# Position scores written to the shift buffer in two halves per unit, and output stores issued by GpSimd

## The reference

```python
xn  = layernorm(x)
out = x + attention(xn) + mlp(xn)

# attention: 16 heads of width 8, with its own layer norm (ln_g, ln_b)
content = einsum('bihd,bjhd->bhij', q + u_bias, k)
pos     = relative_shift(einsum('bihd,jhd->bhij', q + v_bias, p))   # p = sinusoidal_pe(512) @ Wp
attn    = softmax((content + pos) * 8 ** -0.5)
head    = einsum('bhij,bjhd->bihd', attn, v); return head @ Wo + bo

# relative_shift: pad a zero column in front, read the rows of S+1 numbers as one stream, skip the first S of it
padded = concatenate([zeros(B, H, S, 1), pos_score], -1).reshape(B, H, S + 1, S)
return padded[:, :, 1:].reshape(B, H, S, S)

# mlp: three products with weights +1 or -1 (from booleans), relu between, scales s0, s1, s2
h = relu(s0 * [x, -x] @ K0) * 2; h = relu(s1 * h @ K1) * 2; return s2 * h @ K2
```

## Time and profile before

| what | value |
|---|---|
| median of 3 runs | 1502.39 us (1499.39 to 1502.62) |
| profiled execution's own time | 1495.67 us |
| its span, first to last instruction | 1493.8 us |
| mean granted TensorE clock | 0.969 |
| busy: PE, DVE, ACT, POOL | 93%, 86%, 78%, 46% of the span |
| moved by DMA | 575.12 MB, 98,719 packets, mean 385 GB/s |

### The profile page before, as it was taken

How to read it: one execution, slowest core, us unless ns; L and a number is a source line. 1 busy time by engine, 2 the same in 40 slices (tenths; PEclk the granted TensorE clock), 3 DMA queues, 4 the chain that set the end, 5 groups by cost and what they waited for, 6 DMA issues and landing times.

```text
span 1493.8 us, 40812 instructions
## 1 busy us (share of the span) xinstructions
PE 1384.0 (93%) x15848; PEld 940.0 (63%) x15848; DVE 1289.7 (86%) x3479; ACT 1169.9 (78%) x1272; POOL 683.3 (46%) x919
## 2 busy tenths in 40 slices
PE   4898999989899898989999899998989999898997
PEld 2466666666566666656666666666667666666664
DVE  4698898989799898989989899898989989888885
ACT  3687888878688887878878787887878878787863
POOL 5563544535454463544635453463544535443300
PEclk8699999999999999999999999999999999999999
DMA  3999999999999999999999999999999999999991
GB/s 116 363 420 413 384 410 402 406 408 394 378 394 411 399 408 388 410 409 384 409 392 416 396 401 408 385 406 389 409 408 395 415 400 412 382 406 410 389 414 58
DMA packets 98719, 575.12 MB, mean 385 GB/s; under 512 B 15456, under 2 KB 16224, under 8 KB 32992
## 3 DMA queue, kind: packets, MB, share of 16 engines
q1 hardware_dynamic: 42800, 277.83, 47.4%
q10 hardware_dynamic: 37296, 269.51, 44.5%
q0 software_dynamic: 18432, 25.19, 5.7%
HBM read 274.14 MB, written 273.15 MB: 366 GB/s over the span
## 4 chain that ended last, share of the span: by engine, by line
PE 65%; DMA 22%; ACT 6%; issue 2%; DVE 2%; ACTq 1%; POOL 1%; POOLq 0%
PE ps_pt L701 26%; DMA shift<-pos_sb 21%; PE ps_av L715 12%; PE ps_job L646 11%; PE ps_pos L682 10%; ACT pt_sb L456 4%; ACT pos_sb L446 2%; PE ps_job L625 1%; PE ps_job L616 1%; PE ps_job L611 1%; ACTq L433 1%; PE ps_job L621 1%; PE ps_job L607 1%; DMA sc_sb<-shift 1%; DVE sc_sb L581 1%
## 5 line engine op out<-in xcount | busy, mean ns | idle before, releaser
L581 DVE CUSTOM_DVE_ANT_0 sc_sb<-ps_con,sc_sb 128x512 f32<-128x512 f32 x1024 | 664.8, 684 | 135.0 <-PE ps_con L692 124.6
L446 ACT COPY pos_sb<-ps_pos 128x1024 f32<-128x1024 f32 x510 | 519.0, 1018 | 241.8 <-PE ps_pos L682 155.2
L701 PE MATMUL ps_pt<-c_sb,sc_sb 128*128 128x128 f32 x4096 | 566.6, 282 | 31.6 <-ACT pt_sb L456 18.2
L456 ACT ACTIVATE pt_sb<-ps_pt 128x1024 f32<-128x1024 f32 x512 | 526.1, 1028 | 45.5 <-PE ps_pt L701 45.1
L589 DVE TENSOR_SCALAR sc_sb<-sc_sb,nmax 128x512 f32<-128x512 f32 x1024 | 555.8, 575 | 0.1
L701 PEld LDWEIGHTS ps_pt<-c_sb,sc_sb 128*128 128x128 f32 x4096 | 446.3, 142 | 165.8 <-issue 88.1
L341 POOL CAST h<-act_sb 128x512 fp32r<-128x512 f32 x128 | 78.5, 613 | 541.2 <-ACT act_sb L422 541.0
L715 PE MATMUL ps_av<-pt_sb,v_sb 128*9 128x128 f32 x8192 | 321.9, 275 | 0.6 <-ACT pt_sb L456 0.6
L682 PE MATMUL ps_pos<-p_stack,q_stack 32*128 32x512 f32 x1024 | 263.6, 505 | 58.1 <-ACT pos_sb L446 51.5
L715 PEld LDWEIGHTS ps_av<-pt_sb,v_sb 128*9 128x9 f32 x8192 | 173.3, 90 | 157.8 <-issue 147.7
L692 PE MATMUL ps_con<-k_stack,q_stack 32*128 32x512 f32 x1024 | 262.6, 501 | 0.0
(11 more groups left out here) (85 smaller groups left out, 702.1 us busy)
## 6 DMA issues: line engine op xcount, KB each, us to landing
shift<-pos_sb SPq DMA_DIRECT2D x256, 1026.0 KB, 11.0
sc_sb<-shift ACTq DMA_DIRECT2D x256, 1024.0 KB, 11.0
q_stack<-q_hl POOLq DMA_DIRECT2D x192, 64.0 KB, 7.5
k_stack<-k_hl POOLq DMA_DIRECT2D x192, 64.0 KB, 7.6
x_sb<-in_x SPq DMA_DIRECT2D x16, 256.0 KB, 14.8
out<-x_sb SPq DMA_DIRECT2D x16, 256.0 KB, 13.8
c_sb<-in_consts ACTq DMA_DIRECT2D x1, 517.0 KB, 4.5
sc_sb<-in_wp ACTq DMA_DIRECT2D x1, 256.0 KB, 5.1
```

Of the source, the lines that this page charges most:

```text
L446: act.copy(to, ps_pos[:, :, :]).then_inc(s_pe, 1)
L456: act.activation(pt_sb[:, 2 * i:2 * i + 2, :], ps_pt[:, :, :], ACT.Exp, scale=-1.0) \
L581: dve.tensor_tensor_reduce(sc_sb[:, m % N_SC, t, :], ps_con[:, k, :], sc_sb[:, m % N_SC, t, :], -SCALE, 3.4e38, ALU.add, ALU.min, nmax[:, ...
L701: last = pe.transpose(ps_pt[:, j % 2, t * P:(t + 1) * P], sc_sb[:, u % N_SC, t, j * P:(j + 1) * P], id_sb)
```

## The change

SP writes each unit in two transfers of two places each: the first (places 0 and 1) as soon as half step 2n+1 is copied, the second (places 2 and 3) one step later, at the time at which the whole unit was written before. In a step the second half of unit n-1 is issued ahead of the first half of unit n. There are two semaphores for each room of `pos_sb`, one for each half; ACT waits for both before it reads a unit back, and for one of them before it fills place 0 or place 2 again. The stores of the output go from SP to GpSimd's program (`store`), at half step 2 of the batch after next, ahead of the spread of k, and the last one at the end. `load_x` stays on SP, with its wait for the store.

```diff
--- before.py
+++ after.py
@@ -145,7 +145,7 @@
         s_ps = sem("s_ps")
         s_pos, s_con = sem("s_pos"), sem("s_con")
         s_pe = sem("s_pe")
-        s_out_w = [sem(f"s_pout{i}") for i in range(N_POS)]
+        s_out_w = [[sem(f"s_pout{i}_{k}") for k in range(2)] for i in range(N_POS)]
         s_in = [sem(f"s_in{i}") for i in range(N_SC)]
         s_ttr = sem("s_ttr")
         s_sub = sem("s_sub")
@@ -262,6 +262,18 @@
                 sp.dma_start(x_sb[:, b % N_X].rearrange("p t d -> p (t d)"), chunks(x[b].rearrange("s d -> (s d)"))) \
                   .then_inc(s_x[b % N_X], 16)
 
+            def write(u, k):
+
+                if not 0 <= u < UNITS:
+                    return
+                if u >= N_SHIFT:
+                    v = u - N_SHIFT
+                    sp.wait_ge(s_in[v % N_SC], 16 * (v // N_SC + 1))
+                part = slice(2 * k * PITCH, 2 * (k + 1) * PITCH)
+                sp.dma_start(chunks(shift[u % N_SHIFT])[:, :, part],
+                             pos_sb[:, u % N_POS, 2 * k:2 * k + 2].rearrange("p t c -> p (t c)")) \
+                  .then_inc(s_out_w[u % N_POS][k], 16)
+
             load_x(0)
             for dst, src in ((k0_u8, k0), (k1_u8, k1), (k2_u8, k2)):
                 sp.dma_start(dst, src.rearrange("(a p) n -> p a n", p=P)).then_inc(s_wb, 16)
@@ -269,24 +281,12 @@
 
             for n in STEPS:
                 it, slot = n // 16, n % 16
-                if it >= 2 and slot == 1:
-                    sp.wait_ge(s_jev, job("TY", it - 2))
-                    sp.dma_start(chunks(out[it - 2].rearrange("s d -> (s d)")),
-                                 x_sb[:, (it - 2) % N_X].rearrange("p t d -> p (t d)")).then_inc(s_out, 16)
                 if 0 <= it and it + 2 < B and slot == 4:
                     load_x(it + 2)
-                u = unit(n, 1)
-                if u is not None:
-                    sp.wait_ge(s_pe, score_halves(2 * u + 3))
-                    if u >= N_SHIFT:
-                        v = u - N_SHIFT
-                        sp.wait_ge(s_in[v % N_SC], 16 * (v // N_SC + 1))
-                    sp.dma_start(chunks(shift[u % N_SHIFT]),
-                                 pos_sb[:, u % N_POS].rearrange("p t c -> p (t c)")) \
-                      .then_inc(s_out_w[u % N_POS], 16)
-            sp.wait_ge(s_jev, job("TY", B - 1))
-            sp.dma_start(chunks(out[B - 1].rearrange("s d -> (s d)")),
-                         x_sb[:, (B - 1) % N_X].rearrange("p t d -> p (t d)")).then_inc(s_out, 16)
+                if 0 <= n <= UNITS:
+                    sp.wait_ge(s_pe, score_halves(2 * n + 1))
+                    write(n - 1, 1)
+                    write(n, 0)
             sp.wait_ge(s_out, 16 * B)
 
         @block.gpsimd
@@ -353,6 +353,11 @@
                 for third, part in enumerate(thirds):
                     pool.dma_start(stack[third:P:4, g, :], hl[32 * g:32 * g + 32, part, :]).then_inc(landed[g], 16)
 
+            def store(b):
+                pool.wait_ge(s_jev, job("TY", b))
+                pool.dma_start(chunks(out[b].rearrange("s d -> (s d)")),
+                               x_sb[:, b % N_X].rearrange("p t d -> p (t d)")).then_inc(s_out, 16)
+
             scales(0)
             pool.wait_ge(s_c, 16)
             for h in HALVES:
@@ -363,6 +368,8 @@
                     if h == -8:
                         pool.wait_ge(s_fill, 2)
                     spread(h // 8 + 1, QS, q_hl, (0, 0, 1), s_qh, s_q)
+                if h % 32 == 2 and 2 <= h // 32 <= B:
+                    store(h // 32 - 2)
                 if h % 8 == 2:
                     spread(h // 8, KS, k_hl, (0, 1, 0), s_kh, s_k)
                 if h == 5:
@@ -374,6 +381,7 @@
                 b = batch_at(h, NORM_Z)
                 if b is not None:
                     norm(b, 1)
+            store(B - 1)
 
         @block.scalar
         def _(act):
@@ -428,7 +436,8 @@
             for h in HALVES:
                 u, i = half_of(h, SHIFT_H)
                 if i == 0:
-                    act.wait_ge(s_out_w[u % N_POS], 16 * (u // N_POS + 1))
+                    act.wait_ge(s_out_w[u % N_POS][0], 16 * (u // N_POS + 1))
+                    act.wait_ge(s_out_w[u % N_POS][1], 16 * (u // N_POS + 1))
                     wait(act, s_pt, 2 * (u - N_SC + 1))
                     act.dma_start(sc_sb[:, u % N_SC].rearrange("p t c -> p (t c)"),
                                   chunks(shift[u % N_SHIFT, S:S + S * S])) \
@@ -437,8 +446,8 @@
                 if todo:
                     act.wait_ge(s_pos, score_halves(h))
                     for u, t in todo:
-                        if t == 0 and u >= N_POS:
-                            act.wait_ge(s_out_w[u % N_POS], 16 * (u // N_POS))
+                        if t % 2 == 0 and u >= N_POS:
+                            act.wait_ge(s_out_w[u % N_POS][t // 2], 16 * (u // N_POS))
                     to = [pos_sb[:, u % N_POS, t, 1:PITCH] for u, t in todo]
                     if len(to) == 2:
                         to = bass.AP(tensor=to[0].tensor, offset=to[0].offset,
```

## The result

The changed kernel takes 1720.58 us (median of 4 runs, 1718.87 to 1725.99) against 1501.72 us for the kernel before beside it (median of 4). The ratio of all runs is 1.1466, 95% interval 1.1437 to 1.1495. That is 219 us slower; forecast were 23.

A forecast was written before the change was run, and what follows sets the result against it. The prediction took the DMA engines' time as the bound. Its terms, 25 - 3 + 1 = +23 us on the profiled 1495.67, gave 1518.7, about 1525 us as a median of runs; range 1488 to 1558 us.

The forecast's parts named there:

- Packets: the term that decides: Halved writes on SP's queue add 36,864 packets at 11 ns each over 16 engines: +25 us, bounds 0 and 46.
- Packets cost more: Rival: packets cost 20 to 27 ns, as writes from and to odd addresses; +46 to +62, 1546 to 1562 us, chance 0.14.
- the bound: DMA engines' time is the kernel's length from about 45 to about 1460 us; more DMA time lengthens it one for one.
- for a DMA share of 1 nothing more can be moved: In the steady stretches, share 1.02 or 1.03 at 394 to 404 GB/s, the engines were taken to be at their limit.
- a shorter wait at full engines gives nothing: ACT's wait for a unit's write may shorten, but at constant DMA time that does not shorten the kernel.
- the prediction's estimate with it: Per-packet overhead plus extra access for starts off 256 B: 3.5 to 13 ns a packet, a sum of 8 to 30 us.
- the rival with a transfer's fixed part: Rival: each write's fixed 2.1 us shows, 256 x 2.1 = 538 us if nothing hid it; 2040 us, chance 0.01.
- its 512 issues: SP's 256 more issues of 0.518 us, 133 us, fit beside 1262 us of waiting: cost 0 while the backlog covers it.
- a store held it: Each of 16 stores holds GpSimd some 0.5 to 2.1 us, covered by its waits: cost 0, plus 1 us at the end.
- The ends: At start and end of the kernel, half writes going sooner save time: -3 us, bounds 0 to -5.
- its named wait: ACT's waits for the write of `shift` from `pos_sb` were to go up by some 20 us.
- It becomes faster: Rival: at ACT's stall before the copy, long writes stand in the way; halving them gives 1472 us, chance 0.15.

The follow-up runs named there:

- aligned halves: Kernel before with each unit's write cut into two transfers at the old time, pieces of 4,096 B at multiples of 4,096 B: 1531.74 us against 1526.62.
- pieces of 4,112 B: Kernel before with two transfers of two places at the old time, row pitch 514 numbers, gapless, starts at multiples of 16: 1530.85 us against 1500.87.
- two transfers by partitions: Kernel before with each unit's write cut into two transfers of 64 partitions, rows of 8,208 B kept, at the old time: 1567.06 us against 1512.05.
- even cut: Changed kernel with each row cut into 4,096 B and 4,112 B, all starts multiples of 16: 1592.41 us, 1.037 times the kernel before.
- slow halves: Writes cut into 4,104 B pieces: changed kernel with stores on SP, 1793.92 us; kernel before with both halves at the old time, 1824.93 us.

## Why the prediction was wrong

**What failed: the step "Packets: the term that decides".** It made the price a property of the packet's size, 11 ns each, from rows whose packets all went from DRAM into the chip's memory, or within it, at even addresses. No row of before shows a write that starts 8 past a multiple of 16. Measured, the term is (219 + 3 - 1) x 16 / 36,864 = 96 ns a packet, nearly five times the upper bound (20 ns); yet the aligned halves have the same 36,864 packets for 5 us. So no price per packet was the term: it was the DRAM address at which the cut makes pieces start. On one chip, moving the cut by 8 B takes 1874.87 to 1592.41 us: 282 of the 345 us over the kernel before (82%) belong to the cut's address. The other 62 us would be 27 ns for each added packet; whether they are packets, transfers or the edges at multiples of 16 B, the runs don't agree (aligned halves +5, pieces of 4,112 B +30, two transfers by partitions +55).

The rival "Packets cost more" did name odd addresses, with a chance of 0.14. Its price, 20 to 27 ns, was less than a third of what was measured, since it came from rows of small packets and not of odd ones. That its upper end is the 62 us of the even cut is chance: the even cut has no odd start.

**What held: the bound.** The DMA share is 1.02 to 1.04 in every stretch of 100 us shown here, fast and slow, and the time goes with the GB/s. But that "for a DMA share of 1 nothing more can be moved" holds for the share alone: at these shares the kernels moved 321 to 408 GB/s. That a shorter wait at full engines gives nothing is not shown. The even cut, with its earlier halves and shorter last transfer, is slower than the kernel before, but it has more packets too; and of the slow halves on one chip, the earlier ones took 31 us less.

**The rules that were weighed.** The Trainium skill, "DMA: Bandwidth & Descriptors", "How a descriptor splits into AXI transactions", has an extra access for a start that is not on 256 B, and tells it of bytes that are fetched; the prediction's estimate with it was at most 13 ns a packet. The trace agrees with the direction only. By that rule a start 16 past costs as one 8 past does; measured are +30 us (multiples of 16) and +313 (8 past) for the halves, on two chips, each against its own kernel before, and there the measurement decides. The rule of the Trainium skill, same title, of at least 1 MiB per DMA, section "Rules for kernel authors", would have given the rival with a transfer's fixed part; in the backlog two transfers by partitions cost 0.21 us each and not 2.1.

**The rest of the sum.** The issues of the changed kernel as the earlier trace rows, and one store on GpSimd:

```profile
L273 SPq DMA_DIRECT2D shift<-pos_sb x512: 517/568/1348, 23.4 to 1664.3; - x171
L442 ACTq DMA_DIRECT2D sc_sb<-shift x256: 520/521/587, 42.3 to 1678.8; - x128
```

```profile
843.08 0.60 POOL L358 DMA_DIRECT2D out<-x_sb  x1
```

SP: its 512 issues, 0.568 us in the median, stayed beside its waits. GpSimd: a store held it 0.60 us, inside 0.5 to 2.1, and moving the stores alone measures 1.0043, against 0 in the sum. The ends: the first half left at 23.4 us (before 28.8), but the first read at 42.3 (before 41.1), and the last read 14.5 us behind the last write (before 12.6), so the 3 us that the ends were to give did not show. ACT: its named wait rose by 32 us where 20 were forecast, with the 173.5 us of no named releaser on top. The sign of the whole was right, but by a mechanism that stood in a rival and not in the sum, and the rival "It becomes faster" fell at the point that it named: the rate of the steady stretches went down.

## What to carry to other kernels

When the DMA engines are full, look at where each written piece starts in DRAM before counting packets: here a cut that leaves starts at odd multiples of 8 B cost 313 us, where cuts at multiples of 16 cost 5 and 30, each against its own kernel before. A cut 8 B earlier kept the same plan and removed four fifths of the loss. A share of 1 says who is the bound, and only GB/s beside it says how well it works.

## What the runs showed of the hardware that was not expected

- Writes whose rows all start 8 B past a multiple of 16 in DRAM bring the whole core's DMA rate from about 400 GB/s to about 350, with identical packets and bytes. The reads' packets take longer too (47.0 us per MB against 39.5), though nothing about them was changed.
- Cutting 8 KB rows into two aligned 4 KB packets costs 5 us in 1527 (one run each): there the packet count is all but free.
- The loss by odd starts differs between chips for the changed kernel (1.147 and 1.224 times the kernel before), and hardly for the whole rows moved by 8 B (1.124, and 1.134 in one run); the kernel before stays within 1501 to 1535 us.
- Whole rows at multiples of 8,192 B took 1493.24 us, 33 us less than the kernel before beside them (one run each), and rows of 8,200 B 0.977 times; both read from the slot's start. Neither does the shift, so neither is a version to use.
